# The first layer's rounded copy: written by ScalarE from the accumulator, or by VectorE from memory

## The chip, the core and the metric

The kernel runs on one core of one Trainium2 chip. A core has five engines that work side by side, each through its own queue of instructions in order: TensorE (PE: matmuls into the accumulator memory PSUM; PEld: its weight loads), VectorE (DVE), ScalarE (ACT), GpSimd (POOL) and SyncE (SP, which issues transfers). They wait for each other on semaphores: counters that one engine raises and another waits on. The metric is device time in microseconds (us) of one execution; the kernel before took 6532.46 us (median of 3 runs, 6529.53 to 6537.09).

## What is computed

Two rounds of a graph layer followed by a feed-forward layer on 12500 nodes of 256 features. The part that matters here is the first feed-forward layer: every node goes through 8 experts, each of them three 256x256 layers, and the 8 results are summed with the node's softmax weights.

```python
h = jnp.einsum('bfd,edh->bfeh', x, W1) + b1
h = jax.nn.relu(_bn(h, g1, be1, m1, v1))
h = jnp.einsum('bfeh,ehk->bfek', h, W2) + b2
h = jax.nn.relu(_bn(h, g2, be2, m2, v2))
y = jnp.einsum('bfeh,ehd->bfed', h, Wo) + bo
return jnp.einsum('bfed,fe->bfd', y, w)
```

## The kernel before

Work is done in stages, one behind the other. The stage that is changed, `attend_mix`, runs from about 545 to 3478 us and fuses two things: the summing of the first graph layer (edges in slots of 5 or 4 tiles of 128 edges; one slot for each step) and the three expert layers. It takes the nodes in 49 groups (`q`) of 256 and, in each group, the 8 experts in 8 steps (`e`). All loops are written out, and the order in which each engine's body function calls the pieces is the order of its queue.

TensorE multiplies in a reduced 32-bit format (fp32r). To keep the precision, an operand is held in two parts (class `Split`): `high`, the value rounded to fp32r, and `low`, the rest, value minus `high`. A product is then three matmuls (high by low, low by high, high by high), so a layer of one step is 12 matmuls of 256 columns.

For each step the first layer goes as follows. TensorE's `layer1(q, e)` writes the accumulator `ps1` (names in the trace: `m_ps`, also for the second layer's). ScalarE's `relu1` reads it in two halves, applies scale, bias and relu, writes `hf1` (`mh_full`) in plain 32 bits and raises `h1_ok`. VectorE's `low_h1` waits for that, copies `hf1` into `h1.high` (the CAST of line 1320, `mh_high<-mh_full`), then writes `h1.low` (line 521, `mh_low`) and raises `h1_low`. TensorE's `layer2(q, e)` waits for `h1_low`. There is one `ps1` and one `hf1`; `h1` has two buffers. So `layer1` of the next step waits for `h1_ok` of this step, since `ps1` must have been read out, and `relu1` of the next step waits for `h1_low` of this one.

For the second layer, `relu2` already writes both parts from the accumulator: four instructions, `high` and `full` for each half (line 1633), and VectorE's `low_h2` only subtracts. `low_h1` and `low_h2` have the same line 521 in the trace.

The queues around this place, for one group. TensorE: `layer1(0)`, then for e = 0 to 7: `layer1(e+1)` (for 0 < e < 7), `hand_out` (`m_psE`), `layer3` of two steps ago (`m_psY`), `layer2(e)`, `sum_up` (`m_acc`). Step 0 differs, in this order: `hand_out`, `layer3`, `sum_up`, `output_bias` (`m_psT`), `layer1(1)`, `layer2(0)`. Step 1 begins with `layer1(2)`. So only there two first layers have nothing between them but one second layer. ScalarE: `relu1(0)`, a copy for `output_bias` (line 1649), a copy of a sum, then for each e `relu1(e+1)` and `relu2(e)`. VectorE in each step: `low_h1(e)`, the slot's selection matrix (`m_ST`), `low_h2(e-1)`, the weighing of the slot's edges (`m_f`, `m_V`), a second selection matrix (`m_S`) and the sum over experts (`macc`). GpSimd fetches the edges' rows.

The wait that the text speaks of stands in `layer1`, ahead of its matmuls:

```python
def layer1(q, e):
    at_least(pe, h1_ok, q.n * NX + e)
    for m in range(KB):
        last_i = products_of(nc, ps1[:, m * T2:(m + 1) * T2], ...
    last_i.then_inc(p1_ok, 1)
```

Of the kernel before, what the change touches and what calls it, by code (L numbers as in the profile page):

```python
# [12 lines left out]
ACT = mybir.ActivationFunctionType  # L13
# [11 lines left out]
NX = 8  # L25
# [49 lines left out]
def build(nc, a, out, scratch):  # L75

    top = ExitStack()
    with top:
# [36 lines left out]
        with ExitStack() as first:  # L115
            k["W1"], k["W2"], k["Wo"] = (Split(sbuf, first, f"m{n}", [P, NX, KB, D]) for n in ("W1", "W2", "Wo"))
            k["Wr"] = sbuf(first, "mWr", [P, KB, NX])
            k["bo"] = sbuf(first, "mbo", [NX, D])
            k["br"] = sbuf(first, "mbr", [P, NX])
            k["bn_s"] = [sbuf(first, f"bn_s{i}", [P, NX * KB]) for i in range(2)]  # L120
            k["bn_b"] = [sbuf(first, f"bn_b{i}", [P, NX * KB]) for i in range(2)]
            k["q"] = sbuf(first, "q", [P, NT + 1, 2 * H])
            k["corr"] = sbuf(first, "corr", [P, NT, H])
            with ExitStack() as early:
                k["sd"] = sbuf(early, "sd", [P, NT, 2 * H])
                k["amax"] = sbuf(early, "amax", [P, H])
                k["over_row"] = sbuf(early, "over_row", [1, P])
                phase(prepare, a, k, scratch)
                phase(project_attention, a, k, scratch)
                phase(bounds, a, k, scratch)  # L130
                phase(overflow, k, scratch)
            phase(attend_mix, a, k, scratch)
# [945 lines left out]
def at_least(eng, one, count):  # L1078

    if not (isinstance(count, int) and count <= 0):  # L1080
        eng.wait_ge(one, count)


def attend_mix(nc, a, k, scratch, ctx, sem, sbuf, psum):
# [7 lines left out]
    T2 = GM * P  # L1092
    W1, W2, Wo, Wr, bo, br = (k[n] for n in ("W1", "W2", "Wo", "Wr", "bo", "br"))
    bn_s, bn_b, corr = k["bn_s"], k["bn_b"], k["corr"]
# [22 lines left out]
    hf1, hf2 = (sbuf(ctx, f"m{n}_full", [P, KB, T2]) for n in ("h1", "h2"))  # L1117
# [11 lines left out]
    h1 = [Split(sbuf, ctx, f"mh1{i}", [P, KB, T2]) for i in pair]  # L1129
    h2 = [Split(sbuf, ctx, f"mh2{i}", [P, KB, T2]) for i in pair]  # L1130
    ps1, ps2, psY, psT = (psum(ctx, "m_" + n) for n in ("ps1", "ps2", "psY", "psT"))
# [3 lines left out]
    def s_(name):  # L1135
        return sem(ctx, "m_" + name)
# [11 lines left out]
    p1_ok, h1_ok, p2_ok, h2_ok, y_ps, y_ok = map(s_, ("p1_ok", "h1_ok", "p2_ok", "h2_ok", "y_ps", "y_ok"))  # L1148
    x2_out = [s_(f"x2_out{i}") for i in pair]
    filled = s_("filled")  # L1150
    h1_high, XT_low, h1_low, h2_low = map(s_, ("h1_high", "XT_low", "h1_low", "h2_low"))

    def groups(eng, body):

        for n in range(Q):
            body(Group(n, n // 2, n % 2), n > 0, n < Q - 1)
# [8 lines left out]
    with nc.Block() as block:  # L1165
# [92 lines left out]
        def _(v):  # L1258
# [54 lines left out]
            def low(x, full, ready, at, done):  # L1313

                v.wait_ge(ready, at)
                x.lower(nc, full[:, :, :]).then_inc(done, 1)

            def low_h1(q, e):
                v.wait_ge(h1_ok, q.n * NX + (e + 1))
                nc.vector.tensor_copy(h1[e % 2].high[:, :, :], hf1[:, :, :]).then_inc(h1_high, 1)  # L1320
                low(h1[e % 2], hf1, h1_high, q.n * NX + (e + 1), h1_low)

            def low_h2(q, e):
                low(h2[e % 2], hf2, h2_ok, q.n * NX + (e + 1), h2_low)
# [119 lines left out]
            def body(q, before, after):  # L1444

                for e in range(NX):
                    if e:
                        low_h1(q, e)
# [8 lines left out]
                    if e == 0:  # L1457
                        if before:
                            add(q.prev(), NX - 2)
                        low_h1(q, 0)  # L1460
                        build_S(Slot(q, e + 2))
                        start_sum(q)
# [144 lines left out]
        @block.scalar  # L1607
        def _(s):
            def copy_sum(at, q, j):

                if not at.exists:
                    return
                s.wait_ge(summed, at.a + 1)
                at_least(s, x1_ok, q.n)
                nc.scalar.copy(U[:, j, :], ps_acc[at.par][:, 0:NA]).then_inc(U_ok, 1)

            def relu1(q, e):
                s.wait_ge(p1_ok, q.n * NX + (e + 1))
                at_least(s, h1_low, q.n * NX + e)
                for m in range(KB):  # L1620
                    c = e * KB + m
                    ins = nc.scalar.activation(hf1[:, m, :], ps1[:, m * T2:(m + 1) * T2], ACT.Relu,  # L1622
                                               bias=bn_b[0][:, c:c + 1], scale=bn_s[0][:, c:c + 1])
                ins.then_inc(h1_ok, 1)

            def relu2(q, e):
                s.wait_ge(p2_ok, q.n * NX + (e + 1))
                at_least(s, y_ps, q.n * NX + e - 1)
                at_least(s, h2_low, q.n * NX + e)
                for m in range(KB):  # L1630
                    c = e * KB + m
                    for part in (h2[e % 2].high, hf2):
                        ins = nc.scalar.activation(part[:, m, :], ps2[:, m * T2:(m + 1) * T2], ACT.Relu,  # L1633
                                                   bias=bn_b[1][:, c:c + 1], scale=bn_s[1][:, c:c + 1])
                ins.then_inc(h2_ok, 1)

            def copy_turned(q, to, full, ready, done):
                s.wait_ge(ready, q.n + 1)
                for part in (to.high, full):
                    ins = nc.scalar.copy(part[:, :, :].rearrange("p b t -> p (b t)"), psT[:, :])  # L1640
                ins.then_inc(done, 1)

            def exps(q):
                s.wait_ge(ls_in, q.n + 1)
                nc.scalar.activation(lg[q.par][:, :, :], lg[q.par][:, :, :], ACT.Exp).then_inc(le_ok, 1)

            def copy_weights(q):
                s.wait_ge(wT_ps, q.n + 1)
                nc.scalar.copy(wT[q.par][:, :, :].rearrange("e t p -> e (t p)"), psT[0:NX, 0:T2]).then_inc(wT_ok, 1)

            copy_sum(Slot(starts[0], 3), g0, 0)
            copy_sum(Slot(starts[0], 7), g0, 1)
            copy_turned(g0, XT[0], XF, T_ok, XT_ok)
            exps(g0)
            copy_sum(Slot(starts[1], 3), Group(1, 0, 1), 0)

            def body(q, before, after):
                relu1(q, 0)
                copy_weights(q)
                copy_sum(Slot(q, -1), q.next(), 1)  # L1660
                for e in range(NX):
                    if e + 1 < NX:
                        relu1(q, e + 1)
                    if e == 7 and after:
                        exps(q.next())
                    relu2(q, e)
                    if e == 4:
                        copy_sum(Slot(q, 3), q.next().next(), 0)
                    if e == 5 and after:
                        copy_turned(q.next(), XT[1 - q.par], XF, T_ok, XT_ok)  # L1670
            groups(s, body)
# [868 lines left out]
```

## Time and profile before

| | |
|---|---|
| median of 3 runs | 6532.46 us |
| the profiled execution: its time, its span | 6535.86 us, 6534.1 us |
| fused stage `attend_mix` | about 545 to 3478 us |
| busy over the span: PE, PEld, DVE, ACT, POOL | 79%, 71%, 64%, 27%, 63% |
| busy in the stage (2932 us): PE, DVE, ACT, POOL | 2923, 2632, 1243, 1997 us |

The span is the time from the first to the last instruction of the profiled execution. A row of a list of instructions gives its start and its length in us, the engine, the line, the operation, what it writes and reads, and how many alike were merged in it (x2); in square brackets stands how long the engine was idle just before, and what ended that. Matmuls overlap: one of 256 columns is shown about 0.28 us long, and the next starts about 0.12 us later, so a merged pair (x2) shows 0.40. Start times of neighbouring pairs tell the pace.

### The profile page before, as it was taken

The page shows a single profiled execution, that of the slowest core. Times are in us where ns is not written, and L with a number is a line of the kernel's source. Part 1 is how long each engine was busy: PE and PEld are TensorE (multiplying, and loading weights), DVE is VectorE, ACT ScalarE, POOL GpSimd, SP SyncE. Part 2 cuts the span into 40 slices and gives each one's busy share as a digit, 9 for nine tenths or more (in the row PEclk, how much of TensorE's full clock was granted, in tenths as well). Part 3 has the DMA queues.
Part 4 walks back from the last instruction along what each step waited for, and adds up shares of the span by engine and source line. Part 5 has one row for each costly group of instructions (what it writes and reads, how often), then busy time and mean ns, then how long its engine had stood idle before and what let it go on. Part 6 is the DMA issues. An engine that isn't in the chain of part 4 may idle for free. (4 is left out here: it accounts for less than half of the span.)

```text
span 6534.1 us, 98546 instructions
## 1 busy us (share of the span) xinstructions
PE 5150.2 (79%) x32067; PEld 4637.9 (71%) x32068; DVE 4163.5 (64%) x9813; ACT 1761.5 (27%) x4052; POOL 4122.6 (63%) x4039
## 2 busy tenths in 40 slices
PE   4438999999999999999995666666666666665887
PEld 3328999999999999999994554554455555455887
DVE  6437899899899889989983333343343343334666
ACT  2202444444444444444441000000000000003554
POOL 1357766776777767677654777777777777771111
PEclk9658999999999999999997777777777777787999
DMA  6555555555555565556543444444444444443121
GB/s 190 151 151 150 152 159 151 154 157 150 155 156 155 149 154 159 150 153 159 150 121 92 128 134 127 128 134 126 125 130 123 121 124 119 118 120 107 64 77 49
DMA packets 639144, 877.37 MB, mean 134 GB/s; under 512 B 254782, under 2 KB 447376, under 8 KB 638050
## 3 DMA queue, kind: packets, MB, share of 16 engines
q0 software_dynamic: 183392, 501.66, 27.2%
q1 hardware_dynamic: 424972, 334.16, 19.6%
q10 hardware_dynamic: 30326, 35.87, 1.6%
q8 instruction: 239, 3.92, 0.2%
q14 instruction: 215, 1.76, 0.1%
HBM read 766.70 MB, written 155.49 MB: 141 GB/s over the span
## 5 line engine op out<-in xcount | busy, mean ns | idle before, releaser
L1231 POOL DMA_INDIRECT m_ring<-tab_a,m_src x1764 | 1970.2, 1117 | 849.5 <-issue 489.4
L1849 POOL DMA_INDIRECT eb_rows<-tab_b,eb_src x1764 | 1714.9, 972 | 541.2 <-issue 537.0
L2090 PE MATMUL eb_acc<-eb_rows,eb_S 128*128 128x257 f32 x3528 | 1131.9, 492 | 505.6 <-DMA eb_rows<-tab_b,eb_src 504.4
L2090 PEld LDWEIGHTS eb_acc<-eb_rows,eb_S 128*128 128x128 f32 x3528 | 884.5, 256 | 714.6 <-DMA eb_rows<-tab_b,eb_src 530.8
L1512 PE MATMUL m_acc<-m_V,m_S 128*128 128x264 f32 x3528 | 862.5, 390 | 0.0
L1916 DVE TENSOR_TENSOR eb_sum<-eb_acc,eb_sum 128x257 f32<-128x257 f32 x98 | 41.8, 426 | 1232.2 <-PE eb_acc L2090 1232.2
L1512 PEld LDWEIGHTS m_acc<-m_V,m_S 128*128 128x128 f32 x3528 | 648.4, 192 | 93.0
L1633 ACT ACTIVATE mh_high<-m_ps,bn_b,bn_s 128x256 fp32r<-128x256 f32 x784 | 441.5, 563 | 891.7 <-PE m_ps L533 891.7
L521 DVE TENSOR_TENSOR mh_low<-mh_full,mh_high 128x512 fp32r<-128x512 f32 x784 | 543.3, 693 | 63.8 <-ACT mh_full L1633 49.6
L1622 ACT ACTIVATE mh_full<-m_ps,bn_b,bn_s 128x256 f32<-128x256 f32 x784 | 400.6, 563 | 664.5 <-DVE mh_low L521 342.0
L1307 DVE TENSOR_TENSOR m_V<-m_ring,m_V 128x1280 f32<-128x1280 f32 (+1 forms) x392 | 532.8, 1359 | 13.4
L1499 PEld LDWEIGHTS m_psE<-q,m_ST 128*128 128x128 f32 x3528 | 439.4, 195 | 54.4 <-DVE m_ST L1276 49.5
L2168 ACT COPY rGT<-r_ps_g 128x512 f32<-128x512 f32 x98 | 52.8, 588 | 1572.5 <-PE r_ps_g L2100 1572.5
L1499 PE MATMUL m_psE<-q,m_ST 128*128 128x16 f32 x3528 | 429.8, 256 | 45.9 <-DVE m_ST L1276 45.9
L1633 ACT ACTIVATE mh_full<-m_ps,bn_b,bn_s 128x256 f32<-128x256 f32 x784 | 441.3, 563 | 0.0
L1276 DVE TENSOR_SCALAR m_ST<-m_dstb,m_col 128x640 f32<-128x640 int32 (+1 forms) x392 | 410.5, 1047 | 10.3 <-DMA m_dstb<-dst_p 5.8
L2303 POOL DMA_INDIRECT out_dram<-xYR,xtok x76 | 74.7, 983 | 513.1 <-DVE xYR L2356 501.5
L1414 DVE SCALAR_TENSOR_TENSOR macc<-m_psY,mwg,macc 128x256 f32<-128x256 f32 x784 | 341.2, 477 | 79.1 <-PE m_psY L533 78.3
L533 PE MATMUL m_ps<-mXT_low,mW_high 128*128 128x256 f32 x1568 | 373.6, 320 | 0.0
L1898 DVE TENSOR_TENSOR eb_S<-eb_nodes,eb_dst 128x1152 f32<-128x1152 f32 x196 | 258.8, 1361 | 162.9 <-DMA eb_dst<-dst_p 161.2
L533 PE MATMUL m_psY<-mWo_low,mh_high 128*128 128x256 f32 x1568 | 343.2, 300 | 6.4 <-DVE macc L1414 6.4
L533 PE MATMUL m_ps<-mh_low,mW_high 128*128 128x256 f32 x1568 | 318.6, 284 | 1.9 <-ACT mh_full L1633 1.3
(367 smaller groups left out, 10539.9 us busy)
## 6 DMA issues: line engine op xcount, KB each, us to landing
m_dstb<-dst_p SPq DMA_DIRECT2D x196, 320.0 KB
m_dstb<-dst_p SPq DMA_DIRECT2D x196, 256.0 KB
buf<-empty SPq DMA_DIRECT2D x49, 771.0 KB
m_ring<-tab_a,m_src POOLq DMA_INDIRECT x1764
eb_rows<-tab_b,eb_src POOLq DMA_INDIRECT x1764, 2.8
xw_stage<-in_L_ffn_w_dram ACTq DMA_DIRECT2D x16, 1024.0 KB, 9.0
over<-b_blank SPq DMA_DIRECT2D x9, 1452.0 KB, 15.3
mOV<-over SPq DMA_DIRECT2D x49, 264.0 KB, 4.8
```

The costliest lines, as they stand in the source:

```text
L521: return nc.vector.tensor_tensor(low, full, high.bitcast(FP32), SUB)
L533: last = nc.tensor.matmul(out, x[i], y[j], start=n == 0, stop=n == len(steps) - 1)
L1231: gp.indirect_dma_start(out=ring[:, j, :], out_offset=None, in_=scratch["tab_a"], in_offset=bass.IndirectOffsetOnAxis(ap=src[:, j:j + 1], ...
L1276: nc.vector.tensor_scalar(ST[s.side][:, 0:s.size, :], dstb[s.side][:, 0:s.size * P].rearrange("q (p c) -> q c p", c=s.size), node_col[s.pa ...
L1307: nc.vector.tensor_tensor(to[:, 0:size, 0:D].rearrange("p t (h o) -> p t h o", h=H), got[:, :, 0:D].rearrange("p t (h o) -> p t h o", h=H) ...
L1414: nc.vector.scalar_tensor_tensor(acc[p][:, j, :], psY[:, j * D:(j + 1) * D], wg[p][:, j, e:e + 1], acc[p][:, j, :], MUL, ADD).then_inc(y_o ...
L1499: last_i = nc.tensor.matmul(psE[s.side][:, j * 16:j * 16 + 2 * H], ST[s.side][:, j, :], k["q"][:, s.n, :], start=True, stop=True)
L1512: last_i = nc.tensor.matmul(ps_acc[s.par][:, 0:NA], S[:, s.first + j, :], V[s.side][:, j, :], start=s.first + j == 0, stop=s.first + j == ...
L1622: ins = nc.scalar.activation(hf1[:, m, :], ps1[:, m * T2:(m + 1) * T2], ACT.Relu, bias=bn_b[0][:, c:c + 1], scale=bn_s[0][:, c:c + 1])
L1633: ins = nc.scalar.activation(part[:, m, :], ps2[:, m * T2:(m + 1) * T2], ACT.Relu, bias=bn_b[1][:, c:c + 1], scale=bn_s[1][:, c:c + 1])
L1849: gp.indirect_dma_start(out=rows_[q.par][j][:, t, 0:D], out_offset=None, in_=scratch["tab_b"], in_offset=bass.IndirectOffsetOnAxis(ap=src_ ...
L2090: last_i = nc.tensor.matmul(ps_acc[j][:, 0:NR], S[q.par][j][:, t, :], rows_[q.par][j][:, t, :], start=t == 0, stop=t == WT - 1)
```

## The change

`relu1` now writes `h1.high` and `hf1` from the accumulator, as `relu2` does: four instructions on ScalarE in each step instead of two. `low_h1` no longer copies; it waits for `h1_ok` and subtracts. The semaphore between the copy and the subtraction, `h1_high`, is gone.

```diff
             def low_h1(q, e):
                 v.wait_ge(h1_ok, q.n * NX + (e + 1))
-                nc.vector.tensor_copy(h1[e % 2].high[:, :, :], hf1[:, :, :]).then_inc(h1_high, 1)
-                low(h1[e % 2], hf1, h1_high, q.n * NX + (e + 1), h1_low)
+                h1[e % 2].lower(nc, hf1[:, :, :]).then_inc(h1_low, 1)
...
                 for m in range(KB):
                     c = e * KB + m
-                    ins = nc.scalar.activation(hf1[:, m, :], ps1[:, m * T2:(m + 1) * T2], ACT.Relu,
-                                               bias=bn_b[0][:, c:c + 1], scale=bn_s[0][:, c:c + 1])
+                    for part in (h1[e % 2].high, hf1):
+                        ins = nc.scalar.activation(part[:, m, :], ps1[:, m * T2:(m + 1) * T2], ACT.Relu,
+                                                   bias=bn_b[0][:, c:c + 1], scale=bn_s[0][:, c:c + 1])
                 ins.then_inc(h1_ok, 1)
```

ScalarE's queue at the start of a group, from the copy for `output_bias` on: `relu1(1)` (line 1622), `relu2(0)` (line 1633), `relu1(2)`. Before:

```order
L1649 COPY mwT<-m_psT 8x256
L1615 COPY mU<-m_acc 128x264
L1622 ACTIVATE mh_full<-m_ps,bn_b,bn_s 128x256 x2
L1633 ACTIVATE mh_high<-m_ps,bn_b,bn_s 128x256
L1633 ACTIVATE mh_full<-m_ps,bn_b,bn_s 128x256
L1633 ACTIVATE mh_high<-m_ps,bn_b,bn_s 128x256
L1633 ACTIVATE mh_full<-m_ps,bn_b,bn_s 128x256
L1622 ACTIVATE mh_full<-m_ps,bn_b,bn_s 128x256 x2
```

The same place of ScalarE's queue now:

```order
L1649 COPY mwT<-m_psT 8x256
L1614 COPY mU<-m_acc 128x264
L1622 ACTIVATE mh_high<-m_ps,bn_b,bn_s 128x256
L1622 ACTIVATE mh_full<-m_ps,bn_b,bn_s 128x256
L1622 ACTIVATE mh_high<-m_ps,bn_b,bn_s 128x256
L1622 ACTIVATE mh_full<-m_ps,bn_b,bn_s 128x256
L1633 ACTIVATE mh_high<-m_ps,bn_b,bn_s 128x256
L1633 ACTIVATE mh_full<-m_ps,bn_b,bn_s 128x256
L1633 ACTIVATE mh_high<-m_ps,bn_b,bn_s 128x256
L1633 ACTIVATE mh_full<-m_ps,bn_b,bn_s 128x256
```

Two instructions were added to each `relu1`, ahead of `relu2` of the step before; `h1_ok` is raised by the fourth instead of the second. (Lines behind the copy are one lower.)

VectorE's queue at the same time, from the start of the sum over experts (`macc<-mR,m_psT`) on: `low_h1(1)`, a selection matrix, `low_h2(0)`, the weighing. Before:

```order
L1402 TENSOR_TENSOR macc<-mR,m_psT 128x512
L1320 CAST mh_high<-mh_full 128x512
L521 TENSOR_TENSOR mh_low<-mh_full,mh_high 128x512
L1276 TENSOR_SCALAR m_ST<-m_dstb,m_col 128x512
L521 TENSOR_TENSOR mh_low<-mh_full,mh_high 128x512
L1301 TENSOR_TENSOR m_f<-m_psE,m_ring 128x64
```

The same place of VectorE's queue now:

```order
L1401 TENSOR_TENSOR macc<-mR,m_psT 128x512
L521 TENSOR_TENSOR mh_low<-mh_full,mh_high 128x512
L1276 TENSOR_SCALAR m_ST<-m_dstb,m_col 128x512
L521 TENSOR_TENSOR mh_low<-mh_full,mh_high 128x512
L1301 TENSOR_TENSOR m_f<-m_psE,m_ring 128x64
```

The CAST is gone, once in each step, and the subtraction behind it now waits for ScalarE itself. TensorE's queue has the same instructions in the same order as before.

## Rows read from the trace of the kernel before

**Rows 1.** Busy us (count) of PE, PEld, DVE, ACT, POOL; granted clock, DMA, GB/s: fused stage.

```profile
546.00:3478.00 2932.00, 2923.49 (x21728) 2776.11 (x21727) 2632.45 (x5221) 1243.25 (x2639) 1996.92 (x1879) 1.00 0.57 150
```

**Rows 2.** What PE waited for in the fused stage: us in total, times, longest us.

```profile
PE m_psY L533 <- DVE macc L1414: 6.4, 2, 4.4
PE m_ps L533 <- ACT mh_full L1633: 1.3, 2, 0.6
PE m_ps L533 <- DVE mh_low L521: 0.6, 2, 0.4
```

**Rows 3.** Two other waits in the fused stage: VectorE's for relu1, PEld's for ScalarE's copy.

```profile
DVE mh_high L1320 <- ACT mh_full L1622: 91.0, 48, 1.9
PEld m_psT L1542 <- ACT mwT L1649: 0.3, 1, 0.3
```

**Rows 4.** The group of the CAST: count, busy us, mean ns of one, idle before and its releasers.

```profile
L1320 DVE CAST mh_high<-mh_full 128x512 fp32r<-128x512 f32 x392 | 174.4, 445 | 91.2 <-ACT mh_full L1622 91.0 <-DVE macc L1402 0.2
```

**Rows 5.** ScalarE in group 24, around steps 0 and 1, in order of time.

```profile
2011.64 1.02 ACT L1622 ACTIVATE mh_full<-m_ps,bn_b,bn_s 128x256 f32<-128x256 f32 x2 [2.30 <-PE m_ps L533]
2013.06 0.56 ACT L1633 ACTIVATE mh_high<-m_ps,bn_b,bn_s 128x256 fp32r<-128x256 f32 x1 [0.39 <-PE m_ps L533]
...
2014.42 0.57 ACT L1633 ACTIVATE mh_full<-m_ps,bn_b,bn_s 128x256 f32<-128x256 f32 x1
```

**Rows 6.** TensorE in the same stretch: layer1(1) ends, layer2(0), layer1(2) begins.

```profile
2011.21 0.40 PE L533 MATMUL m_ps<-mXT_high,mW_high 128*128 128x256 f32 x2
2011.44 0.40 PE L533 MATMUL m_ps<-mh_low,mW_high 128*128 128x256 f32 x2
...
2012.62 0.40 PE L533 MATMUL m_ps<-mh_high,mW_high 128*128 128x256 f32 x2
2012.86 0.40 PE L533 MATMUL m_ps<-mXT_low,mW_high 128*128 128x256 f32 x2
2013.09 0.40 PE L533 MATMUL m_ps<-mXT_high,mW_low 128*128 128x256 f32 x2
```

**Rows 7.** VectorE in the same stretch: the CAST of step 1 and the subtraction.

```profile
2012.69 0.43 DVE L1320 CAST mh_high<-mh_full 128x512 fp32r<-128x512 f32 x1 [1.91 <-ACT mh_full L1622]
2013.15 0.69 DVE L521 TENSOR_TENSOR mh_low<-mh_full,mh_high 128x512 fp32r<-128x512 f32 x1
```

**Rows 8.** The same place in the last group (48): relu1(1), and layer1(2) of TensorE.

```profile
3442.74 1.02 ACT L1622 ACTIVATE mh_full<-m_ps,bn_b,bn_s 128x256 f32<-128x256 f32 x2 [2.84 <-PE m_ps L533]
3443.95 0.40 PE L533 MATMUL m_ps<-mXT_low,mW_high 128*128 128x256 f32 x2
```

**Rows 9.** Group 24: layer2(1) behind the last pair of layer3; relu1(5) and layer1(6).

```profile
2016.54 0.39 PE L533 MATMUL m_psY<-mWo_high,mh_high 128*128 128x256 f32 x2
2016.77 0.39 PE L533 MATMUL m_ps<-mh_low,mW_high 128*128 128x256 f32 x2
...
2037.33 1.02 ACT L1622 ACTIVATE mh_full<-m_ps,bn_b,bn_s 128x256 f32<-128x256 f32 x2 [2.62 <-DVE mh_low L521]
...
2041.47 0.59 PE L533 MATMUL m_ps<-mXT_low,mW_high 128*128 128x256 f32 x2
```

**Rows 10.** TensorE starting again after a wait, twice, with ScalarE's instruction ahead of the second.

```profile
3417.15 0.47 PE L533 MATMUL m_ps<-mh_low,mW_high 128*128 128x256 f32 x2 [0.24 <-DVE mh_low L521]
...
3434.50 0.57 ACT L1633 ACTIVATE mh_full<-m_ps,bn_b,bn_s 128x256 f32<-128x256 f32 x1
...
3435.12 0.51 PE L533 MATMUL m_ps<-mh_low,mW_high 128*128 128x256 f32 x2 [0.65 <-ACT mh_full L1633]
```

**Rows 11.** A long and a short wait of TensorE, and stretches around them (columns as Rows 1).

```profile
587.08 0.79 PE L533 MATMUL m_psY<-mWo_low,mh_high 128*128 128x256 f32 x2 [4.37 <-DVE macc L1414]
586.00:592.00 6.00, 4.92 (x29) 4.92 (x30) 5.90 (x13) 1.02 (x2) 4.80 (x4) 0.72 0.53 166
...
6270.47 0.36 PE L2411 MATMUL x_ps_h<-xxT_low,xw_high 128*128 128x256 f32 x1 [0.94 <-DVE xxT_low L2329]
6240.00:6330.00 90.00, 80.77 (x649) 77.86 (x648) 60.78 (x132) 46.47 (x115) 13.76 (x14) 1.00 0.24 78
```

More of the change, by code:

```diff
@@ L1150, in attend_mix @@
     filled = s_("filled")
-    h1_high, XT_low, h1_low, h2_low = map(s_, ("h1_high", "XT_low", "h1_low", "h2_low"))
+    XT_low, h1_low, h2_low = map(s_, ("XT_low", "h1_low", "h2_low"))
     def groups(eng, body):
```

## The prediction

> **What bounds the kernel now.** I read the busy times of the fused stage first, since the change touches nothing else. TensorE is busy 2923.49 of 2932 us at a granted clock of 1.00 (the 2.4 GHz level), VectorE 2632, ScalarE 1243 [rows 1]. "Busy" alone is not proof for matmuls, which overlap, so I read next what TensorE waited for: 6.4 + 1.3 + 0.6 = 8.3 us in 2932 [rows 2]. And the pace in a list of instructions: pairs of matmuls follow each other every 0.23 to 0.24 us, from one layer into the next without a gap [rows 6]. So TensorE's queue is full from end to end. Two things follow. Taking work from VectorE or ScalarE can win no more than those 8.3 us. And whatever holds TensorE up anew is paid in full, because there is no idle time in the stage that could absorb it. The question is therefore not which engine does the rounding more cheaply, but whether TensorE somewhere waits for `relu1`, which becomes longer.
>
> **What the change takes away.** The CAST goes: 392 times 445 ns, 174 us of VectorE's time [rows 4]. None of it lies on TensorE's path, since TensorE waited for VectorE 6.4 + 0.6 us in all [rows 2]; of these the longest single wait, 4.37 us, comes in the second group and only once [rows 11]. I count the gain as 0. Its bounds are 0 and 7 us.
>
> **What it adds.** Two more instructions in each `relu1`, and `h1_ok` two instructions later. Two such take 1.02 us from the first start to the last end (2011.64 to 2012.66) [rows 5]. Four, written alternately to `high` and `full` and with the same shapes, are what `relu2` already is: 2013.06 to 2014.42 + 0.57 = 2014.99, 1.93 us [rows 5]. So `relu1` becomes 0.91 us longer, 392 times. ScalarE has the room for it (357 us more on 1243 of 2932 [rows 1]); what counts is who waits for the end of `relu1`. There are three.
>
> First, VectorE's `low_h1`. At step 1 it stands waiting for `relu1`: 48 waits of 1.9 us, one in nearly every group [rows 3]; the CAST starts 0.03 us after `relu1` ends [rows 5, 7]. The subtraction started 0.46 us behind the CAST (2013.15) [rows 7] and will come directly, so it starts 0.91 - 0.46 = 0.45 us later there, at 2013.60. `layer2(1)`, which needs it, starts at 2016.77 [rows 9]. Queued behind `low_h1` on VectorE are the selection matrix and the weighing for later slots; they move by the same half microsecond and win 0.46 us back in each further step. Cost 0.
>
> Second, `relu2(0)`, queued behind `relu1(1)` on ScalarE. It started 0.39 us after ScalarE became free [rows 5], so it starts 0.91 - 0.39 = 0.52 us later and ends at 2015.5. `layer2(1)`, which needs `ps2` read out, comes at 2016.77: a cover of 1.3 us is left. Cost 0.
>
> Third, TensorE itself: `layer1(e+1)` waits for `h1_ok(e)`. In most steps much lies between two first layers. In group 24 the shortest such cover is that of step 5: `relu1(5)` ends at 2037.33 + 1.02 = 2038.35, `layer1(6)` starts at 2041.47, 3.1 us later [rows 9]. **Step 1 is the exception.** `layer1(1)` and `layer1(2)` have only `layer2(0)` between them. `relu1(1)` ends at 2012.66, and `layer1(2)` starts at 2012.86, 0.24 us behind the pair in front of it, so without waiting [rows 5, 6]: the cover is 0.20 us. In the last group it is 3443.95 - 3443.76 = 0.19 us [rows 8], and the 48 equal waits of VectorE say that the groups between are alike [rows 3]. Now the sum for one group. With four instructions `relu1(1)` ends at 2011.64 + 1.93 = 2013.57. From ScalarE's end to the matmul's start a waiting TensorE took 0.05 us (3435.07 to 3435.12) [rows 10]. So `layer1(2)` starts at 2013.62 instead of 2012.86: 0.76 us lost. Behind a wait the first pair of matmuls is also slower, since its weights aren't loaded ahead: 0.47 and 0.51 us instead of 0.39 and 0.40, that is 0.08 to 0.11 [rows 6, 9, 10]; I take 0.10. Together 0.86 us a group, and 49 x 0.86 = 42.1 us. `layer1(2)` shifts everything behind it on TensorE, and as TensorE has no slack, nothing gives it back.
>
> One more: ScalarE's copy for `output_bias` stands behind `relu1(0)`. PEld waited for it once, 0.3 us [rows 3]; where it does already, the longer `relu1` adds 0.9 us, once. Total 43.0 us. Bounds: without the restart cost and this last one 49 x 0.76 = 37 us; with the whole 0.91 and 0.11 uncovered 49 x 1.02 + 0.9 = 51 us. I take 43, as its pieces are read at the place itself.
>
> Set on the profiled execution: span 6534.1 + 43.0 = 6577.1 us, its own time 6535.86 + 43.0 = 6578.9 us. That execution lies 3.4 us above the median of the runs, so for the median I take 6532.46 + 43.0 = 6575.5 us.
>
> **A page's price beside it.** The 0.91 us for two more instructions is read from `relu2` [rows 5]. The Trainium skill, "ScalarE: Activation LUTs", What ACT_TABLE_LOAD costs, gives for such an instruction 280 ns + 0.833 ns per column, 93 ns more for the second pointer operand, and 93 ns that two in a row overlap: an estimate from that page of 0.99 us for two, by which the sum would be 49 x 0.08 = 3.9 us larger, 6579 us. The row is 0.08 us shorter, and I keep it.
>
> **The rivals.** *The cover holds.* If TensorE did not have to wait (`relu1` with four no longer than 1.17 us, so that it ends by 2012.81), the time stays at 6532 us. Against it: `relu2`, of the same form, takes 1.93. *Not slower, by faster matmuls.* The 256-column pairs of layers 1 and 2 follow each other every 0.24 us, those behind layer 3 every 0.23 [rows 6, 9]. Were VectorE's traffic the reason and the CAST its part, 392 x 12 pairs x 0.01 = 47 us would come back: 6532 + 43 - 47 = 6528 us. It decides from 0.009 us a pair on. Against it: while VectorE idles for 1.91 us ahead of the CAST, pairs come every 0.23 (2011.21, 2011.44), and under the CAST too (2012.86, 2013.09) [rows 6, 7]. *The clock falls.* After the 4.37 us wait the granted clock was 0.72 over 6 us, so part of it at the 1.2 GHz level: 0.28 x 6 = 1.7 us lost [rows 11]. If each new gap did that, 49 x 1.7 = 83 us come on top: 6659 us. Against it: in the last stage TensorE stops for 0.94 us between busy stretches, longer than the 0.6 us that the new gap leaves between two matmuls' shown times (2012.62 + 0.40 to 2013.62), and the granted clock over 90 us there is 1.00 [rows 11]. The Trainium skill, "TensorE: Matmul & The Clock Gate", A second HAM failure mode: psum-queue depth-cycling, says that short idles between groups of matmuls can make the clock swing; by that rule this rival is the case, and the 1.00 speaks against it here. *A second gap.* If the 0.52 us of `relu2(0)` got through to TensorE in each group, 49 x 0.52 = 25 us more, 6601 us; it would take a cover below 0.52 where 2016.77 - 2014.99 = 1.78 is read [rows 5, 9].
>
> **How the numbers follow.** About 0.2% (13 us) is what a measurement of this kernel can tell from no change. Forecast 0.85; cover holds 0.06; not slower by faster matmuls 0.04 (half of it a clear gain); clock 0.03; second gap 0.02. The range takes the bounds 37 and 51 us with some 4 us for the spread of the runs: 6563 to 6587, nearly all of the forecast's 0.85 and nothing of the others. Faster 0.02; same 0.06 + 0.02 = 0.08; slower 0.85 + 0.03 + 0.02 = 0.90.
>
> **What would show it.** In the changed kernel's trace: TensorE's waits get a new row, `m_ps` waiting for `relu1`, 49 times about 0.6 us as idle time is counted (a matmul's shown length covers part of the gap), against none now. At step 1 `layer1(2)` starts some 2.0 us after `relu1(1)` starts instead of 1.2; at the other steps nothing changes. VectorE's busy time in the stage falls by about 174 us and its idle time grows by that and the stage's lengthening; the stage lasts about 43 us longer, every other stage as long as before. I am wrong if that row is missing, if it has far fewer or more than 49 entries, or if the granted clock in the stage falls below 1.00.

## The result, and the profile after

The changed kernel takes 6568.45 us (median of 5 runs, 6563.15 to 6577.26) against 6532.46 us before: a ratio of 1.0055 with a 95% interval of 1.0041 to 1.007, so 36 us or 0.55% slower (27 to 46 us). The forecast was 6575.5 us, 43 us slower, with a range of 6563 to 6587. The profiled execution took 6563.15 us, the shortest of the five, with a span of 6561.4 us.

The answers to [rows 1, 2] are the busy times of the fused stage in the kernel after (up to 3500 us; the stage now ends at 3510.8) and what TensorE waited for in the whole stage (columns as there):

```profile
546.00:3500.00 2954.00, 2922.36 (x21648) 2766.68 (x21647) 2455.47 (x4813) 1593.32 (x3409) 2064.47 (x1875) 1.00 0.56 149
```

```profile
PE m_ps L533 <- ACT mh_full L1622: 29.6, 49, 0.6
PE m_psY L533 <- DVE macc L1413: 2.2, 2, 2.0
PE m_ps L533 <- ACT mh_full L1633: 1.3, 2, 0.7
PE m_psT L1541 <- ACT mwT L1649: 1.0, 1, 1.0
PE m_psT L1528 <- ACT mXT_full L1640: 0.2, 1, 0.2
```

The first row of the waits is new: TensorE's first layer waits for `relu1` (line 1622) 49 times. 48 of them are `layer1(2)` in the groups 0 to 47, 0.6 us each as idle time is counted. The 49th stands elsewhere, in group 47, where `layer1(5)` waits for `relu1(4)`:

```profile
3447.88 0.51 PE L533 MATMUL m_ps<-mXT_low,mW_high 128*128 128x256 f32 x2 [0.29 <-ACT mh_full L1622]
```

The last two groups have no `hand_out` and no `sum_up` left between two first layers, and the cover at this place of group 47 was 0.47 us in the kernel before (3418.12 to 3418.59), about half of what `relu1` grew by:

```profile
3417.10 1.02 ACT L1622 ACTIVATE mh_full<-m_ps,bn_b,bn_s 128x256 f32<-128x256 f32 x2 [1.00 <-DVE mh_low L521]
...
3418.59 0.39 PE L533 MATMUL m_ps<-mXT_low,mW_high 128*128 128x256 f32 x2
```

In the last group (48) `layer1(2)` also waits, but too short to be counted: TensorE itself came late there. The fourth row is the wait for the copy behind `relu1(0)`, in the last group alone; for the weight loads it grew from the 0.3 us of [rows 3] to 1.2 us, and TensorE's matmuls now show 1.0.

The granted clock is 1.00 over the stage, and no gap at step 1 of the groups 0 to 47 is followed by a lower one. It fell once, in the last group, some 1.6 us after that wait of 1.03 us had ended, to the 1.2 GHz level (columns as [rows 1]):

```profile
3472.00:3475.40 3.40, 3.40 (x18) 3.40 (x17) 0.33 (x1) 1.40 (x4) 0.00 (x0) 0.50 0.00 0
```

From `layer1(1)` to `layer1(2)` the last group became 1.58 us longer, where the groups 1 to 47 became 0.77 longer. The 1.03 us wait alone doesn't settle it: it also stands in two of the kernels below (without step 1, and with six instructions), and no such stretch followed in them; in two others (with more cover, and with three instructions) one did.

The same place as [rows 5, 6, 7], group 24: `relu1(1)` on ScalarE and `relu2(0)` behind it, then the end of `layer2(0)` and the start of `layer1(2)` on TensorE, then VectorE's subtraction of step 1.

```profile
2020.89 0.56 ACT L1622 ACTIVATE mh_high<-m_ps,bn_b,bn_s 128x256 fp32r<-128x256 f32 x1 [2.30 <-PE m_ps L533]
...
2022.26 0.57 ACT L1622 ACTIVATE mh_full<-m_ps,bn_b,bn_s 128x256 f32<-128x256 f32 x1
2022.71 0.58 ACT L1633 ACTIVATE mh_high<-m_ps,bn_b,bn_s 128x256 fp32r<-128x256 f32 x1
```

```profile
2021.87 0.40 PE L533 MATMUL m_ps<-mh_high,mW_high 128*128 128x256 f32 x2
2022.88 0.50 PE L533 MATMUL m_ps<-mXT_low,mW_high 128*128 128x256 f32 x2 [0.61 <-ACT mh_full L1622]
2023.22 0.40 PE L533 MATMUL m_ps<-mXT_high,mW_low 128*128 128x256 f32 x2
```

```profile
2022.86 0.69 DVE L521 TENSOR_TENSOR mh_low<-mh_full,mh_high 128x512 fp32r<-128x512 f32 x1 [2.83 <-ACT mh_full L1622]
```

`relu1(1)` now lasts from 2020.89 to 2022.83, 1.94 us. TensorE's last pair of `layer2(0)` starts at 2021.87; the next would have followed at 2022.11 and comes at 2022.88, 0.05 us after ScalarE's end. Its pair takes 0.50 us instead of 0.40; its weight load starts together with its matmul, where in the kernel before it started 0.12 us ahead. VectorE waits at the same spot for 2.83 us (1.91 before), since it has no copy left to do and ScalarE is later.

VectorE's saved time became waiting. Its group of subtractions in the kernel after, line 521 (count, busy us, mean ns, idle time before, releasers):

```profile
L521 DVE TENSOR_TENSOR mh_low<-mh_full,mh_high 128x512 fp32r<-128x512 f32 x784 | 541.3, 691 | 282.6 <-ACT mh_full L1633 142.0 <-ACT mh_full L1622 139.1
```

282.6 us of idle time stand before it now. Before, 63.8 us stood there and 91.2 us before the CAST [rows 4]. Most of the rest is found before the sum over experts (`macc`): 166.3 us instead of 89.0.

### The profile page after: what moved, and what is told of

It is laid out like the page before. It is cut to its first block and busy times, and to the rows that moved or that the text cites. A ratio compares the mean times of both kernels' runs of the same rounds, so it can differ in the third digit from the quotient of the medians.

```text
span 6561.4 us, 98937 instructions
## 1 busy us (share of the span) xinstructions
PE 5157.5 (79%) x32067; PEld 4636.9 (71%) x32068; DVE 3997.1 (61%) x9421; ACT 2118.8 (32%) x4836; POOL 4186.4 (64%) x4039
## 5 line engine op out<-in xcount | busy, mean ns | idle before, releaser
L1231 POOL DMA_INDIRECT m_ring<-tab_a,m_src x1764 | 2000.6, 1134 | 751.6 <-issue 494.0
L521 DVE TENSOR_TENSOR mh_low<-mh_full,mh_high 128x512 fp32r<-128x512 f32 x784 | 541.3, 691 | 282.6 <-ACT mh_full L1633 142.0
L1633 ACT ACTIVATE mh_high<-m_ps,bn_b,bn_s 128x256 fp32r<-128x256 f32 x784 | 444.0, 566 | 765.1 <-PE m_ps L533 743.3
L1622 ACT ACTIVATE mh_high<-m_ps,bn_b,bn_s 128x256 fp32r<-128x256 f32 x784 | 443.1, 565 | 516.1 <-PE m_ps L533 512.7
L1633 ACT ACTIVATE mh_full<-m_ps,bn_b,bn_s 128x256 f32<-128x256 f32 x784 | 444.3, 567 | 0.0
L1622 ACT ACTIVATE mh_full<-m_ps,bn_b,bn_s 128x256 f32<-128x256 f32 x784 | 442.7, 565 | 0.0
```

The lines of the kernel that those rows point to most:

```text
L521: return nc.vector.tensor_tensor(low, full, high.bitcast(FP32), SUB)
L1231: gp.indirect_dma_start(out=ring[:, j, :], out_offset=None, in_=scratch["tab_a"], in_offset=bass.IndirectOffsetOnAxis(ap=src[:, j:j + 1], ...
L1622: ins = nc.scalar.activation(part[:, m, :], ps1[:, m * T2:(m + 1) * T2], ACT.Relu, bias=bn_b[0][:, c:c + 1], scale=bn_s[0][:, c:c + 1])
```

## Experiments

All were timed beside the kernel before on the same chip; ratios are to it.

**The change without step 1.** The change is kept in seven steps; at step 1 VectorE copies and ScalarE writes two instructions, as before.

```diff
-                    for part in (h1[e % 2].high, hf1):
+                    for part in (hf1,) if e == 1 else (h1[e % 2].high, hf1):
...
+                if e == 1:
+                    nc.vector.tensor_copy(h1[e % 2].high[:, :, :], hf1[:, :, :]).then_inc(h1_high, 1)
+                    v.wait_ge(h1_high, q.n + 1)
                 h1[e % 2].lower(nc, hf1[:, :, :]).then_inc(h1_low, 1)
```

> The change is kept in seven of eight steps; at step 1 of each group VectorE copies again and ScalarE writes two instructions. Theory (only step 1, where layer1(2) waits for relu1(1), costs): TensorE's wait for relu1 is gone from its list, and the time is that of the kernel before or up to 5 us less, 6527 to 6535 us. Rival (ScalarE's longer work costs something in every step): seven eighths of the 36 us stay, about 6564 us.

Measured: 6530.74 us against 6529.52, ratio 1.0005 (0.9996 to 1.0014). TensorE's waits for `relu1` (line 1625 in this kernel) in the stage up to 3470 us:

```profile
PE m_psY L533 <- DVE macc L1416: 2.6, 1, 2.6
PE m_ps L533 <- ACT mh_full L1636: 1.3, 2, 0.7
...
PE m_ps L533 <- ACT mh_full L1625: 0.3, 1, 0.3
```

One wait for `relu1`, of 0.3 us, stands where 49 stood; it is the one in group 47. Seven eighths of the added ScalarE work cost nothing that can be measured, and seven eighths of the removed copies win nothing: from the start of one step's first layer to that of the next, averaged over the groups 2 to 45, no interval differs from the kernel before by 0.001 us.

**The change at step 1 alone.**

```diff
-                    for part in (h1[e % 2].high, hf1):
+                    for part in (hf1,) if e != 1 else (h1[e % 2].high, hf1):
```

with VectorE's copy in the other seven steps.

> The change is made at step 1 alone; in the other seven steps the kernel is as before. Theory: the whole loss is there, 49 waits of 0.6 us of idle time and 0.8 to 0.87 us of delay each, 6532 + 39 to 43 = 6571 to 6575 us, and not less than the changed kernel. Rival (a cost in every step): an eighth of the 36 us, about 6537 us.

Measured: 6565.54 us against 6529.52, ratio 1.0064 (1.0051 to 1.0078), 36.0 us more. An eighth of the added instructions makes the whole loss. The median lies below the 6571 to 6575 us expected, but the interval, 33 to 51 us, holds the 39; in the profiled executions the fused stage is 38.6 us longer.

**The whole change, with more cover on TensorE.** At step 1 `hand_out` goes ahead of `layer1(2)`.

```diff
+                    if e == 1:
+                        hand_out(Slot(q, e + 1))
                     if 0 < e < NX - 1:
                         layer1(q, e + 1)
-                    hand_out(Slot(q, e + 1))
+                    if e != 1:
+                        hand_out(Slot(q, e + 1))
```

> The whole change, but TensorE's hand_out of step 1 (8 or 10 matmuls, about 1.1 us, whose inputs lie ready for some 8 us) stands ahead of layer1(2) instead of behind it. Theory: the cover at step 1 grows from 0.2 to about 1.3 us, more than the 0.91 us that relu1 grew; TensorE's wait for relu1 vanishes and the time is that of the kernel before or a few us less, 6525 to 6535 us. Rival (ScalarE's longer work costs elsewhere too): above 6545 us. If the order itself harmed something, a new row in TensorE's waits would show it.

Measured: 6531.33 us against 6529.52, ratio 1.0004 (0.9995 to 1.0013). ScalarE is as long at step 1 as in the changed kernel, but in group 24 its last instruction and TensorE's queue around it read so (`relu1` is line 1625 in this kernel):

```profile
2006.08 0.57 ACT L1625 ACTIVATE mh_full<-m_ps,bn_b,bn_s 128x256 f32<-128x256 f32 x1
```

```profile
2005.69 0.40 PE L533 MATMUL m_ps<-mh_high,mW_high 128*128 128x256 f32 x2
2005.93 1.18 PE L1498 MATMUL m_psE<-q,m_ST 128*128 128x16 f32 x10
2006.96 0.49 PE L533 MATMUL m_ps<-mXT_low,mW_high 128*128 128x256 f32 x2
```

`relu1(1)` ends at 2006.65 and `layer1(2)` begins at 2006.96 without a wait: 0.31 us of cover are left. The work that the change added is the same, the loss is gone. It stays in group 47, which has no `hand_out` to move: 0.61 us of waiting and 0.77 us of delay at the same place.

**The order alone.** The kernel before with the same move of `hand_out` (the same diff on it).

> The kernel before, with only TensorE's hand_out of step 1 moved ahead of layer1(2). Theory: TensorE is full either way and nothing waits there, so the time is that of the kernel before, within 5 us. Rival (the order itself is worth something, and hid a loss of ScalarE's longer work in the kernel with both): 10 us or more faster than before.

Measured: 6530.53 us against 6532.56, ratio 0.9994 (0.9985 to 1.0003). So the move by itself is worth nothing that can be told from noise (by the trace 0.067 us a group, 3 us in all) and hid nothing in the run above. Interval by interval the two kernels with the move agree within 0.001 us in the groups 2 to 45: once the cover is there, the change costs these groups nothing, and wins nothing.

**The length of `relu1(1)` as a dial.** Three instructions: VectorE copies the second half at step 1 (its part of the edit is left out here).

```diff
-                    for part in (h1[e % 2].high, hf1):
+                    for part in (hf1,) if e == 1 and m == 1 else (h1[e % 2].high, hf1):
```

> The whole change, but at step 1 ScalarE writes three instructions instead of four: the rounded copy of the second half is made by VectorE there. Theory (relu1's length beyond the cover is lost): relu1(1) is 0.45 us longer than before, the cover takes 0.14 of it, the restart adds 0.10: 49 x 0.41 = 20 us over the kernel before, about 6550 us, and 49 waits of TensorE too short to be counted in full, 0.1 to 0.2 us each. Rival (any wait of TensorE costs a fixed amount, whatever its length): about 6566 us. Rival (nothing is lost below some length): 6530 us.

Measured: 6553.42 us against 6532.56, ratio 1.0032 (1.002 to 1.0045), 20.9 us more. TensorE's wait, and one place of it in group 24:

```profile
PE m_ps L533 <- ACT mh_full L1625: 7.7, 49, 0.3
```

```profile
2014.40 0.40 PE L533 MATMUL m_ps<-mh_high,mW_high 128*128 128x256 f32 x2
2014.95 0.50 PE L533 MATMUL m_ps<-mXT_low,mW_high 128*128 128x256 f32 x2 [0.15 <-ACT mh_full L1625]
```

The list of waits counts 7.7 us where 20.9 are lost. The pair should follow after 0.24 us and comes after 0.55; of these 0.31 us the shown length of the matmul ahead covers 0.16. Both rivals are out: a fixed cost of any wait would have given about 6566 us, no cost of a short one 6530.

Six instructions: two more, one ahead of each pair, into `hf2`, which `relu2` writes anew (two waits of ScalarE that keep `hf2` safe are left out here).

```diff
-                    for part in (h1[e % 2].high, hf1):
+                    for part in ((hf2,) if e == 1 else ()) + (h1[e % 2].high, hf1):
...
```

> The whole change, and at step 1 two more ScalarE instructions ahead of the four (into a buffer that is written again afterwards). Theory: relu1(1) is another 0.91 us longer and all of it is lost, 49 x 0.91 = 44.6 us over the changed kernel, about 6613 us; 49 waits of about 1.5 us. Rival (the granted clock falls behind waits of this length): the same plus up to 83 us, 6695 us, and a granted clock below 1.00 in the stage. Rival (cost by the number of ScalarE instructions): 98 more on 784, about 6573 us.

Measured: 6615.33 us against 6529.52, ratio 1.0136 (1.0121 to 1.0152), 85.8 us more. The waits and the clock of the stage up to 3470 us (it ends at 3560, two groups later):

```profile
PE m_ps L533 <- ACT mh_full L1624: 71.4, 47, 1.5
```

```profile
546.00:3470.00 2924.00, 2852.46 (x21060) 2699.91 (x21061) 2412.50 (x4721) 1576.23 (x3374) 2041.63 (x1870) 1.00 0.55 149
```

Over two, three, four and six instructions the loss is 0, 20.9, 36 and 85.8 us. Per group that is 0, 0.43, 0.73 and 1.75 us, each uncertain by about 0.2. The traces show the place itself more sharply: `relu1(1)` lasts 1.02, 1.48, 1.93 and 2.84 us, and `layer1(2)` starts 0, 0.316, 0.772 and 1.679 us later (average of the groups 2 to 45), in the last three 0.053 us after ScalarE's end. So the loss follows the length of `relu1(1)` beyond the cover, and its rivals here, a cost by the number of instructions (6573 us) among them, are out. Gaps of 1.5 us in every group leave the granted clock at 1.00, so the rival of the falling clock is out even at more than twice the gap.

**VectorE with more work instead of less.** The kernel before, its copy made twice in each step.

```diff
                 nc.vector.tensor_copy(h1[e % 2].high[:, :, :], hf1[:, :, :]).then_inc(h1_high, 1)
-                low(h1[e % 2], hf1, h1_high, q.n * NX + (e + 1), h1_low)
+                v.wait_ge(h1_high, 2 * (q.n * NX + e) + 1)
+                nc.vector.tensor_copy(h1[e % 2].high[:, :, :], hf1[:, :, :]).then_inc(h1_high, 1)
+                low(h1[e % 2], hf1, h1_high, 2 * (q.n * NX + (e + 1)), h1_low)
```

> The kernel before, with VectorE's copy made twice in each step, one behind the other: 392 x 0.46 = 180 us more work on VectorE, ScalarE unchanged. It asks whether VectorE is as far off the path as the change took for granted. If its work is hidden with much room: 6532 us. If VectorE, which is behind from step 2 of a group on, delays h1_low (0.46 us a step, summed up since step 1, against covers of 1 to 3 us in steps 3 to 7): up to 0.8 us a group, 6545 to 6575 us, with a wait of layer2 for mh_low in TensorE's list.

Measured: 6573.23 us against 6532.56, ratio 1.0066 (1.005 to 1.0082), 40.7 us more. TensorE's waits for VectorE in the stage up to 3470 us:

```profile
PE m_ps L533 <- DVE mh_low L521: 3.5, 10, 1.3
PE m_psY L533 <- DVE macc L1416: 3.4, 17, 0.8
```

Taking the copy away wins nothing, but adding one costs 40 us: VectorE has less room than a second copy in each step takes. The named waits make only 6.9 us of it. From the start of one step's first layer to the next's, averaged over groups 2 to 45, nothing changes up to step 4; then 0.12, 0.31, 0.26 and 0.29 us are added in the intervals that begin with the first layers of steps 4 to 7. `layer2` of the steps 3, 4 and 7 begins 0.05, 0.20 and 0.23 us later behind the matmul ahead of it and then takes 0.06 to 0.10 us longer, and `layer3` of step 3 begins 0.25 us later: together nearly all of it. One such place, `layer2(4)` of group 24, with VectorE's subtraction ahead of it:

```profile
2051.89 0.69 DVE L521 TENSOR_TENSOR mh_low<-mh_full,mh_high 128x512 fp32r<-128x512 f32 x1
2052.28 0.39 PE L533 MATMUL m_psY<-mWo_high,mh_high 128*128 128x256 f32 x2
2052.72 0.47 PE L533 MATMUL m_ps<-mh_low,mW_high 128*128 128x256 f32 x2
```

The pair at 2052.72 comes 0.14 us after the subtraction's end and 0.44 us behind the pair ahead of it, where 0.23 is the pace: 0.21 us are lost, and no wait is listed, since the shown length of the matmuls covers most of it. So the loss is waiting for VectorE, mostly in waits that the list does not count.

## Why the prediction was right, point by point

**TensorE is full, and nothing gives a new wait back: right.** Averaged over groups 2 to 45 and taken from the start of one step's first layer to that of the next, the changed kernel differs from the one before in three of eight intervals: +0.772 us from step 1 to step 2, +0.111 from 2 to 3, -0.052 from 3 to 4. The other five differ by less than 0.001.

**The place and the size of the wait: right.** 0.772 us were measured where 0.76 was forecast, and the slower restart where 0.10 was taken is 0.106 of the 0.111, inside `layer1(2)`. (The rest of that interval changes by +0.10 and -0.08 us in alternate groups, by the two paces told of in the last section.) The sum is 0.83 us a group where 0.86 was forecast. The -0.052 was not foreseen (below). That the list has 49 waits, as forecast, is luck: it has 48 at the place that was forecast and one at another.

**The other seven steps and the other two waiters cost nothing: right, but for group 47.** The run without step 1 shows it for the steps. The cover of 3.1 us that the prediction took for them was read in group 24; in group 47, with less work on TensorE, it was 0.47 to 1.1 us in the steps 2 to 5, and steps 4 to 6 there lost 0.3 us. For `relu2(0)`, `layer2(1)` did not wait; `relu2(0)` came only 0.40 us later behind the start of `relu1(1)`, not 0.52, as ScalarE's instructions overlap by 0.12 us back to back. For `low_h1`, VectorE's idle time grew without a trace on TensorE.

**The one wait at the end: right in its size**: from `layer1(0)` to `layer1(1)` the last group is 0.9 us longer, as taken. The low clock that followed it in this execution was in no sum.

**The removed copy wins nothing: right by the experiments; what was off in the sum lies at the ends of the stage.** In the profiled executions the stage (from the first matmul of `layer1` to the last of `layer3`) grew from 2934.8 to 2972.6 us, 37.8 us where 43 was forecast. The groups 1 to 46 make 38.1 of it, 0.83 each. The first group became 4.6 us shorter: the 4.37 us wait of the kernel before [rows 11], which stands in this group and not in the second as the prediction says, is 0.2 us in the changed kernel, and the stretch at a lower clock behind it is gone too. The last two groups became 4.2 us longer, by the gap at step 1, the wait for the copy and the low clock behind that. That these two ends nearly cancel is chance.

Whether the copy's absence shortens that early wait is not shown, and the other kernels speak against it: it was 3.1 us in one that has the copy in every step, 2.8 in one that has it in none, and 0.8 in the one that makes it twice. Outside the stage, which the change does not touch, the same two executions differ as well: ahead of it 543.4 us before and 538.2 after, behind it 3055.9 and 3050.6. So the forecast of the whole time rests on parts that move by some us from one execution to the next, and the 36 us of the medians can't be told from 43.

**The range.** Its lower end is not what its words say: 6532.46 + 37 less 4 us is 6565.5 and not 6563. The measured 6568.45 lies above both.

**The page's price: too high here.** Two more instructions lengthened `relu1` by 0.91 us as in the rows; by the estimate of 0.99 us from the Trainium skill, "ScalarE: Activation LUTs", What ACT_TABLE_LOAD costs, `layer1(2)` would have started 0.85 us later instead of the measured 0.772.

**The rivals.** The cover did not hold. The clock did not fall behind the gaps at step 1; the one fall, in the last group, stands behind another wait. No second gap appeared. Faster matmuls were not brought by the missing CAST: the run without step 1 has seven eighths of the CASTs gone and not one interval changed by 0.001 us. The kernel with the change at step 1 alone, which has the CAST in seven steps, shows the same small gain, 0.112 us a group in the interval from 3 to 4, as the one that only moves `hand_out` in the kernel before, with no CAST removed.

## What to carry to other kernels

When one engine is full, a change on another is judged by the one place where the full engine comes closest to waiting for it: look through one period step by step for the shortest cover, and price that alone. A step that breaks the pattern, as at the start of a loop body, decides here: 49 of 392 occurrences carried nearly the whole loss, and moving 1.1 us of ready work into that spot removed it wherever there was such work. Look at the last periods too: where work runs out, covers shrink that are long everywhere else. A list of waits undercounts short waits of TensorE, because matmuls are shown longer than their pace; start times of neighbouring matmuls tell what is lost.

## What was not expected of the hardware

The 12 matmuls of a second layer kept one of two paces from the second on, and mostly the third layer ahead of them had nearly the same. In group 24 `layer2(2)` of the kernel before, three pairs in order:

```profile
2024.10 0.40 PE L533 MATMUL m_ps<-mh_low,mW_high 128*128 128x256 f32 x2
2024.34 0.40 PE L533 MATMUL m_ps<-mh_high,mW_low 128*128 128x256 f32 x2
2024.57 0.40 PE L533 MATMUL m_ps<-mh_high,mW_high 128*128 128x256 f32 x2
```

The same three of the changed kernel:

```profile
2034.27 0.39 PE L533 MATMUL m_ps<-mh_low,mW_high 128*128 128x256 f32 x2
2034.50 0.39 PE L533 MATMUL m_ps<-mh_high,mW_low 128*128 128x256 f32 x2
2034.73 0.39 PE L533 MATMUL m_ps<-mh_high,mW_high 128*128 128x256 f32 x2
```

Averaged over the layer in group 24 from its second matmul on, a matmul follows the last after 117.8 ns in the one and 113.3 ns in the other, at a granted clock of 1.00 in both. The kernel before has both paces too: its `layer2(1)` takes 113.3 in every second group and 117.8 in the others. Which of the two a run takes changed in the steps behind the new gap and, in other kernels here, behind the moved `hand_out`; the CAST is not its cause. What sets it stays open. Over 24 matmuls it is some 0.10 us. That much is saved between the first layers of steps 3 and 4 in every second group, and it is the small term, 0.052 us on average, by which the measured 0.83 us a group differs from 0.772 + 0.111.
